# A scatter by indirect transfers whose engine waits one chunk further back for a landing

## What is computed

```python
# first layer: 32 experts, 4 for each token, 128 hidden values
logits = flat @ router_w.T + router_bias
scores = softmax(logits)
topk_scores, topk_idx = top_k(scores, 4)            # then divided by their sum
h = silu(flat @ gate_w[e].T) * (flat @ up_w[e].T)   # for every expert e
out = sum over the 4 chosen e of topk_scores[e] * (h @ down_w[e].T)
out = out + silu(flat @ sgate_w.T) * (flat @ sup_w.T) @ sdown_w.T   # shared expert, 512 hidden

# second layer: 8 experts, 2 for each token, 512 hidden values
h = silu(x_flat @ experts_w1[e].T)
out = silu(x_flat @ shared_w1.T) @ shared_w2.T + sum over the 2 chosen e of gate[e] * (h @ experts_w2[e].T)
```

## Time and profile before

| | |
|---|---|
| times of three runs | 1374.3, 1374.77, 1383.91 us |
| median | 1374.77 us |
| span of the profiled execution | 1383.5 us |
| TensorE, products busy | 943.3 us, 68% |
| VectorE busy | 783.1 us, 57% |
| ScalarE busy | 632.5 us, 46% |
| GpSimd busy | 509.7 us, 37% |
| moved over HBM | 45.61 MB read, 50.33 MB written |

### The profile page before, as it was taken

The page is one execution under the profiler, slowest core; times in us unless marked ns, Lnnn a source line. Parts: engine busy times, 40 slices in busy tenths (PEclk is TensorE's granted clock), DMA queues, the critical chain, the costliest instruction groups (busy, mean ns, idle before and its releaser), DMA issues. The chain is left out here.

```text
span 1383.5 us, 19852 instructions
## 1 busy us (share of the span) xinstructions
PE 943.3 (68%) x5650; PEld 715.8 (52%) x5652; DVE 783.1 (57%) x2423; ACT 632.5 (46%) x1304; POOL 509.7 (37%) x634
## 2 busy tenths in 40 slices
PE   3895676643578777986685236777578889978920
PEld 2534555533466666875573013444457757756720
DVE  5497798977634362324574378998864311004535
ACT  3446777748221132422234145676774334534510
POOL 0005555631566665045534742000016460044044
PEclk9996677765599898998896557898878989999965
DMA  7920000014111244544432100000031122122131
GB/s 216 289 85 0 1 0 0 0 37 180 37 44 45 90 129 123 137 119 128 112 107 75 50 25 19 1 0 0 1 139 45 58 74 68 53 70 77 32 84 54
DMA packets 133844, 97.00 MB, mean 70 GB/s; under 512 B 11648, under 2 KB 125696, under 8 KB 132736
## 3 DMA queue, kind: packets, MB, share of 16 engines
q1 hardware_dynamic: 121472, 70.79, 17.3%
q0 software_dynamic: 12288, 25.19, 6.2%
HBM read 45.61 MB, written 50.33 MB: 69 GB/s over the span
## 5 line engine op out<-in xcount | busy, mean ns | idle before, releaser
L1719 DVE COPY e_y_rows<-e_ps_y 128x512 f32<-128x512 f32 x68 | 47.0, 691 | 216.8 <-PE e_ps_y L1293 139.7
L1100 POOL DMA_INDIRECT e_xs<-h_tok,rows_of x128 | 130.1, 1017 | 100.1 <-issue 36.1
L1245 PE MATMUL e_ps_gu<-e_w_all,e_x_turned 128*128 x384 | 113.2, 446 | 52.0 <-ACT e_x_turned L1416 31.3
L1113 POOL DMA_INDIRECT e_got<-e_ys,e_rows_of x64 | 65.9, 1030 | 159.0 <-DMA e_ys<-e_y_rows 125.5
L739 ACT ACTIVATE mask<-ps_q,k_neg 128x256 bf16<-128x256 f32 x256 | 101.0, 489 | 34.9 <-PE ps_q L853 34.9
L1245 PEld LDWEIGHTS e_ps_gu<-e_w_all,e_x_turned 128*128 128x128 f32 x384 | 79.7, 218 | 71.5 <-issue 59.7
L1113 POOL DMA_INDIRECT e_got<-e_ys,rows_of x64 | 65.1, 1017 | 95.7 <-DMA e_ys<-e_y_rows 57.6
L1422 ACT ACTIVATE e_silu<-e_ps_gu 128x512 f32<-128x512 f32 x48 | 28.7, 598 | 154.2 <-PE e_ps_gu L1245 87.7
L1427 ACT ACTIVATE e_hidden<-e_ps_up 128x512 f32<-128x512 f32 x80 | 47.8, 598 | 102.4 <-PE e_ps_up L1275 85.5
L853 PE MATMUL ps_q<-q_parts,pick 128*128 (+1 forms) x256 | 56.7, 360 | 52.1 <-DVE mask L651 46.3
L2207 POOL DMA_INDIRECT c_got<-e_ys,rows_of x64 | 66.6, 1040 | 69.0 <-POOLq L1029 33.6
(11 more groups left out here) (384 smaller groups left out, 2354.4 us busy)
## 6 DMA issues: line engine op xcount, KB each, us to landing
e_x_rows<-e_xs SPq DMA_DIRECT2D x68, 256.0 KB
e_ys<-e_y_rows SPq DMA_DIRECT2D x68, 256.0 KB
e_xs<-zeros SPq DMA_DIRECT2D x2, 6144.0 KB, 34.2
e_w_all<-in_w SPq DMA_DIRECT2D x4, 1536.0 KB
e_xs<-zeros SPq DMA_DIRECT2D x2, 2560.0 KB, 27.4
e_w_all<-in_w SPq DMA_DIRECT2D x4, 1024.0 KB, 8.8
x_tok<-in_x SPq DMA_DIRECT2D x4, 512.0 KB, 6.3
e_xs<-h_tok,rows_of POOLq DMA_INDIRECT x128
```

The source lines that it names most:

```text
L1100: nc.gpsimd.indirect_dma_start(out=xs[part], out_offset=bass.IndirectOffsetOnAxis(ap=rows_of[:, t * K + k:t * K + k + 1], axis=0), in_=til ...
L1113: nc.gpsimd.indirect_dma_start(out=got[t % GB][:, k * P:(k + 1) * P], out_offset=None, in_=ys[part], in_offset=bass.IndirectOffsetOnAxis(a ...
L1245: last = nc.tensor.matmul(ps_gu[n % 2][:, t * 2 * P:(t + 1) * 2 * P], x_turned[n % 2][:, t * P:(t + 1) * P], at(w_all, col, 2 * P), start= ...
```

## The change

Three lines of the scatter's bookkeeping. GpSimd still issues the same transfers in the same order, eight to a chunk (`PACE` is the number of tiles in a chunk, 2 or 4). Behind a chunk it now waits for the landing of the chunk before that one, and behind the first chunk it doesn't wait. Landings are counted on three signals in turn, so chunk c counts on signal c mod 3, and SyncE waits for the last three chunks of a part.

```diff
     XB, YB, GB, LAG = 4, 4, 4 if gated else 8, 6 if gated else 5
+    PACE = 8 // K
...
-        scattered = [plain(f"scattered{i}") for i in range(GROUPS)]
+        scattered = [plain(f"scattered{i}") for i in range(3)]
...
+        def landed(eng, chunk):
+            eng.wait_ge(scattered[chunk % 3], 16 * PACE * K * (chunk // 3 + 1))
...
                         if q == 0:
-                            for g in range(part * GPP, (part + 1) * GPP):
-                                sp.wait_ge(scattered[g], 16 * TPG * K)
+                            for i in range((part + 1) * PT // PACE - 3, (part + 1) * PT // PACE):
+                                landed(sp, i)
...
                         for k in range(K):
                             nc.gpsimd.indirect_dma_start(
                                 out=xs[part], out_offset=bass.IndirectOffsetOnAxis(ap=rows_of[:, t * K + k:t * K + k + 1], axis=0),
-                                in_=tile(h_tok, t), in_offset=None, bounds_check=ROWS - 1).then_inc(scattered[t // TPG], 16)
-                        if (t + 1) * K % 8 == 0:
-                            pool.wait_ge(scattered[t // TPG], 16 * K * (t % TPG + 1))
+                                in_=tile(h_tok, t), in_offset=None, bounds_check=ROWS - 1).then_inc(scattered[t // PACE % 3], 16)
+                        if (t + 1) % PACE == 0 and t >= PACE:
+                            landed(pool, t // PACE - 1)
```

## The result

The changed kernel took 1500.3, 1507.38 and 1522.48 us, beside 1374.3 to 1383.91 of the kernel before on the same chip. The ratio is **1.0985**, with a 95% interval of 1.0924 to 1.1047: 10% slower. (A fourth execution took 2032.61 us, far from the others, and is left out.) The forecast was 1435, range 1370 to 1482: the direction holds, the size doesn't. As the experiments show, size and sign hang on where the runs fell: on another chip the changed kernel takes 1231 us and the kernel before 1237.

The account below looks back on a forecast made before the run. TensorE's chain was taken as the bound, slowed beside GpSimd's transfers, with the scatter's end on no path. Layer 0 +41, layer 1 +10 and +9 summed to +60, about 1435 us against the median of 1374.8, range 1370 to 1482.

Parts of the forecast that it names:

- The moved wait is always met: GpSimd's 22 remaining landing waits in the scatter: cost 0, all inner pauses go, runs of 84 and 41 us.
- SyncE, the three signals, the first scatter of part two cost nothing: Scatter bookkeeping: SyncE's extra waits are hidden, the signals add no instruction, part two waits only for its places; cost 0.
- The end of the scatter is on no path: Both layers: TensorE's first turn of loaded rows waits for VectorE's copy, so a shorter scatter by itself gains nothing.
- A long run halts the others and a pause sets it back: Beside GpSimd transfers other engines slow to 0.2 to 0.4 after seven us; a 2 us pause resets this; chance 0.70.
- 0.35 of free speed behind seven free us: Engines beside each unpaced scatter run: seven free us, then 0.35 speed; layer 0 +41 us, layer 1 +10 and +9.
- bound of 0.21: Slow-state speed from 48 gathers between the expert layers, applied beside the scatters: +91 us, 1466.
- The doubt that the shared units would sink less than the steps: Layer 0: shared experts at 0.5 beside the scatter, expert-tile steps at 0.35, would sum to some +35 us.
- The places near 465: Layer 0: the places of part two come near 465 us instead of 441, 23 us later.
- A: Rival, beside scatters: halts are a fixed price per transfer whatever the pauses; no change, 1375 us; chance 0.13.
- B: Rival, beside scatters: halts are a fixed share of the scatter's running time; -10 us, 1365; chance 0.08.
- C: Rival, in both layers' scatters: the landing wait itself causes the halts; -54 us, 1321; chance 0.03.
- D: Rival, beside long scatter runs: speed falls below 0.21; at 0.1 about +115 us, 1490; chance 0.06.

Follow-up runs that it names:

- experiment 1: Changed kernel, three signals kept, but GpSimd waits behind every eighth transfer for the chunk just issued: 1389.67 us, kernel before 1390.88, ratio 0.9983.
- Experiment 3: Changed kernel with a GpSimd memset behind each scatter transfer, or seven behind every eighth: 1490.62 and 1385.09 us, kernel before 1390.88.
- the table: Kernels pausing after 4, 8 (before), 16 or 64 transfers (changed; 32 in layer 1): with halts 1347.5, 1373.9, 1455.2, 1508.3 us.
- run 5: Not a follow-up run: the words "first run 5 units" mean 5 shared-expert units done up to the end of the changed kernel's first run of 64 transfers.
- fill: Changed kernel with seven small GpSimd memsets behind every eighth scatter transfer: 1385.09 us, kernel before 1390.88.
- after_third: Changed kernel unaltered, run again on a chip without halts: 1230.93 us, kernel before 1237.41, ratio 0.9938.
- fill3: Changed kernel with three small GpSimd memsets behind every eighth scatter transfer: 1230.13 us, on a chip without halts.
- narrow: Changed kernel, each scatter transfer moving half of every row (256 B instead of 512 B): 1228.79 us, on a chip without halts.
- direct: Changed kernel, each scatter a plain transfer to consecutive rows, without a list of places: 1228.09, 1228.79 and 1230.01 us, on chips without halts.
- gpace4: Kernel with three signals, scatters and gathers all waiting for their own landing behind every fourth transfer: 1347.83 us, kernel before 1238.79, without halts.

## Why the prediction was right or wrong

*The moved wait is always met:* right, 0.6 us in 2 waits, runs of 83.8 and 82.2 us (84 forecast) and 42.6 and 40.9 in layer 1 (41).

*SyncE, the three signals, the first scatter of part two cost nothing:* right, experiment 1.

*The end of the scatter is on no path:* right here (the first loads of part one go out at 435.21, TensorE turns them at 590.48 behind VectorE's copy), wrong for chunks of four.

*A long run halts the others and a pause sets it back:* right for chips with halts. Experiment 3 shows that the pause need not end with a landing, and the table shows the length, with the mean rate moving along.

*0.35 of free speed behind seven free us:* wrong, and this is the step that failed. I took it from 16 gathers, because they stand in the same loop, and so from a run of 21 us. The measured speed in the long halts was 0.07 and 0.09 in the shared experts and 0.16 in layer 1's tiles. Nor does the speed fall from 1 to one lower value after 7 us: at sixteen the longest units took 12 to 14 us, at 64 they took 30 to 37. It deepens with the length, and the row of a run of 16 could not give the value for 64. The seven free us were wrong too, the other way: the halts began 29 and 14 to 19 us in. And a third term stood at nothing: the sum lets the others run free as soon as GpSimd stops, while the last halt of each run went on for another 8 and 9 us. From 372 to the end of the first run 5 units (11.4 us of work) were done where the sum has 22, in the second 7 (16) where it has 34; with the 8 and 9 us behind them this makes some 45 of the 50 us that layer 0 lost beyond the 41 forecast. My bound of 0.21 came from 48 gathers beside a stage where TensorE had little to do. By the sum: part one +46.4, not 23; part two +44.9, not 18; layer 1 +13.3 and +16.8, not 10 and 9; 115 us, not 60 (121.4 in these four, less 6.4 given back in the stage between).

*The doubt that the shared units would sink less than the steps:* it was the other way round. They sank most, and the steps of line 1249, on whose row the forecast of "above 8 us" stood, met no scatter at all: the first standstill had pushed them behind it.

*The places near 465:* 487.52. *Remote waits several times those before:* from 350 to 560 us 114.4 us of ScalarE against 46.9, so two and a half times; of VectorE 111.9 against 15.3, seven times.

*Rivals.* A (a fixed price per transfer) falls with the table: each of its kernels has the same 192 scatters. B (a fixed share) falls with it too. C (the landing wait causes the halts) falls with fill, which has no such wait and 1385 us, and with the changed kernel. D, deeper than 0.21, was the case, with a chance of 0.06: at 0.1 it gave +115 and 1490, and the span grew by 115. That the two sums meet is partly luck: by D's working the parts of layer 0 lose some 39 and 37 us and those of layer 1 some 18 each, the measured ones 46.4, 44.9, 13.3 and 16.8, and 6.4 were given back in a stage that D leaves alone. The median is higher, 1507, since the execution profiled was the fastest of three. D should have had far more: between the 0.37 of a run of 16 and the 0.21 of one of 48 the profile itself showed a fall with the length, and for 64 I had taken a value at the upper end of that fall, where its lower end was the bound to start from.

*The other error has no step in the prediction:* it took the halts for a property of the kernel. One chip's trace can't show that it isn't. The 1375 us on that chip are some 137 more than on the others, whose traces hold no halts, and the sign of the change hangs on it. The Trainium skill, SBUF — State Buffer, section "Who interferes with whom", says that DMA and the compute engines don't contend: on a chip without halts the trace agrees (3.76 us a step beside unpaced scatters), on the others the engines do stand still beside the transfers (10 products in place of 55), though no run shows by what. The Trainium skill's advice to wait late, in DMA: Bandwidth & Descriptors, "Rules for kernel authors", is worth 0.6% on the first and costs 10% on the second.

## What to carry to other kernels

Before a wait that looks like idle time is moved, look at what the other engines do in the pause behind it: here 20 pauses of 2 us in which GpSimd issued no transfer were worth 115 us of the others' work on one chip, nearly 6 us each. A price read from a run of length 16 is not the price at 64; where it falls with the length, take the trend's side, not the nearest row. And where a profile shows waits whose releaser is "remote" in a program of one core, measure on a second chip before the kernel is tuned to them: of the pacings tried, the best is a chunk of four on one kind of chip (1347.5 against 1373.9, one execution) and a long one or none on the other (1230.5 with sixteen, one execution, and 1230.9 with none, against 1238.8 and 1237.4). Chunks of eight, the kernel before, lose 1.9% to four on the one and 0.6% to none on the other.

## What the runs showed of the hardware that I had not expected

**Two kinds of chips.** The kernel before takes 1237 to 1241 us on four and 1365 to 1401 on two (and on that of the result, if it was a third). Up to the first scatter the traces of the changed kernel are alike: it starts at 350.09 and 350.2 us. In the stretches read here, what differs is what happens beside GpSimd's transfers.

**TensorE's signals come late.** The trace keeps the times at which signals were raised, apart from the views. In the halt above, the gate's last product ends at 379.79 and its signal is raised at 398.72; the up product's, ended at 380.49, at 406.42. VectorE's own, for an instruction that ends at 407.19, is raised at 407.21. Between 345 and 560 us, with the next raise on record taken as the instruction's own, about two thirds of TensorE's follow its end within 0.02 us and a tenth after some 17 us or more, while more than eight tenths of VectorE's and about eight of ScalarE's follow within 0.02; in after_third, without halts, nearly all of the three do. Some raises are missing from the record, so these shares are rough. Ends of products are modelled, so this doesn't tell whether the product or its signal was late.

**Fewer landings are on record.** The trace of the result holds records of 4,062 signals from DMAs, that of after_third 9,284, for the same transfers. Before the scatter the numbers are equal (272 and 272 in the first 50 us, 400 and 400 from 300 to 350); from 350 to 400 they are 213 and 576. Whether whatever carries or records the signals is overrun there would be a guess; what is shown is that records are missing where the halts are.

**Open.** Whether the kind goes with the chip, since none was used twice. Whether the halts are in the signals' path or in how executions are recorded: every time here is of a recorded one, and the missing records fit either. Whether a pause must outlast the last landing, whether the bytes count, and whether GpSimd's transfers without a list do the same: fill3, narrow and direct ran, but on no chip with halts; nor did gpace4, scatters and gathers in fours. And a kernel with chunks of four in part one and of eight in part two, which would avoid the 27.69 us, was not tried.
